# GNN stack on one core: scattering parked edge sums tile by tile with two under way, instead of four at a time

## What is computed

```python
# L0: relational layer, L1: attention, L2: two SAGE layers, L3: GCN
def sage_mean(x, src, dst, W_self, W_neigh, bias, n):
    s = segment_sum(x[src], dst, n)
    cnt = segment_sum(ones, dst, n)
    return x @ W_self.T + (s / maximum(cnt, 1)[:, None]) @ W_neigh.T + bias
# L3
msgs = (x @ W)[src] * (dis[src] * dis[dst])[:, None]
out = segment_sum(msgs, dst, n)
```

## Time and profile before

| | |
|---|---|
| median of 3 runs | 4481.74 us (4466.53 to 4487.24) |
| profiled execution, its own time | 4498.36 us |
| its span | 4496.7 us |
| busy share of the span | PE 65%, PEld 57%, DVE 56%, ACT 43%, POOL 55% |
| three stretches in which scatters and node part run together | 2413 to 2806 us, 3219 to 3692 us, 4084 to 4482 us |

### The profile page before, as it was taken

How to read it: one execution, slowest core, us unless ns; L and a number is a source line. 1 busy time by engine, 2 the same in 40 slices (tenths; PEclk the granted TensorE clock), 3 DMA queues, 4 the chain that set the end, 5 groups by cost and what they waited for, 6 DMA issues and landing times.

```text
span 4496.7 us, 81538 instructions
## 1 busy us (share of the span) xinstructions
PE 2929.0 (65%) x19724; PEld 2566.6 (57%) x19724; DVE 2499.0 (56%) x11513; ACT 1955.0 (43%) x5394; POOL 2473.3 (55%) x2379
## 2 busy tenths in 40 slices
PE   6888887774656563004767777566777665777666
PEld 5887886663555553003655555466666554666666
DVE  5666667885555453883324555323466563445666
ACT  2222325664544442113546555223444444556555
POOL 5565553666788886445554555545444435554444
PEclk9999998998877776556888676778888887889989
DMA  4444436875333333992113767211277771114767
GB/s 160 157 166 156 163 127 192 239 239 157 41 41 41 41 41 75 313 310 77 38 36 112 229 218 220 71 31 34 86 245 239 230 241 49 37 38 137 221 216 220
DMA packets 328251, 638.77 MB, mean 142 GB/s; under 512 B 61072, under 2 KB 89776, under 8 KB 321992
## 3 DMA queue, kind: packets, MB, share of 16 engines
q1 hardware_dynamic: 233406, 501.99, 34.5%
q0 software_dynamic: 90944, 133.85, 13.2%
q10 hardware_dynamic: 3786, 1.65, 0.1%
HBM read 371.35 MB, written 277.50 MB: 144 GB/s over the span
## 4 chain that ended last, share of the span: by engine, by line
PE 16%; DMA 13%; issue 11%; POOL 10%; another core or an unknown queue 4%; DVE 4%; ACT 3%; SPq 0%; POOLq 0%; DVEq 0%; ACTq 0%
DMA sums<-parked,last_i 12%; POOL sums L774 9%; PE bank L1201 6%; PE bank L1197 3%; PE bank L1185 3%; PE bank L1167 2%; DVE out_stats L1665 1%; PE bank L1137 1%; ACT e_h L911 1%; DVE out_mv L1672 1%; ACT out_sd L1072 1%; ACT psum_out L948 1%; DVE n_t L1765 0%; POOL got L739 0%
## 5 line engine op out<-in xcount | busy, mean ns | idle before, releaser
L774 POOL DMA_INDIRECT sums<-parked,last_i x588 | 603.5, 1026 | 702.6 <-DMA sums<-parked,last_i 506.4
L739 POOL DMA_INDIRECT got<-rows,gidx x588 | 602.7, 1025 | 404.8 <-ACT e_h L911 188.4
L948 ACT ACTIVATE psum_out<-bank 128x132 f32<-128x132 f32 x784 | 219.7, 280 | 939.3 <-remote 455.0
L1201 PE MATMUL bank<-psum_out,eq 128*128 128x132 f32 x1568 | 387.2, 332 | 246.0 <-ACT psum_out L948 154.6
L1033 ACT ACTIVATE n_h<-ring 128x128 f32<-128x128 f32 x1176 | 482.9, 482 | 143.7 <-DMA ring<-rows 71.2
L1302 PE MATMUL bank<-ring,ident 128*128 128x128 f32 x2352 | 507.6, 302 | 0.0
L1201 PEld LDWEIGHTS bank<-psum_out,eq 128*128 128x128 f32 x1568 | 271.2, 216 | 306.4 <-ACT psum_out L948 181.9
L1299 PE MATMUL bank<-w_t,n_ht 128*128 128x128 f32 x1568 | 355.7, 353 | 136.1 <-DMA ring<-sums 135.3
L1277 PE MATMUL bank<-ident,n_h 128*128 128x128 f32 x1176 | 226.9, 324 | 330.9 <-ACT n_h L1033 248.2
L1182 PE MATMUL bank<-parked 128*128 128x128 f32 x3136 | 409.7, 283 | 32.7 <-issue 26.1
L1182 PEld LDWEIGHTS bank<-parked 128*128 128x128 f32 x3136 | 386.9, 199 | 41.4 <-issue 40.6
(11 more groups left out here) (182 smaller groups left out, 7292.4 us busy)
## 6 DMA issues: line engine op xcount, KB each, us to landing
ring<-sums SPq DMA_DIRECT2D x392, 264.0 KB
ring<-rows SPq DMA_DIRECT2D x392, 264.0 KB
rows<-ring SPq DMA_DIRECT2D x294, 264.0 KB
ring<-attsums SPq DMA_DIRECT2D x98, 264.0 KB
rowsg<-ring SPq DMA_DIRECT2D x98, 264.0 KB
ring<-rowsg SPq DMA_DIRECT2D x98, 264.0 KB
sums<-parked SPq DMA_DIRECT2D x16, 1584.0 KB
attsums<-parked SPq DMA_DIRECT2D x16, 1584.0 KB
```

Source lines behind the costliest of these rows:

```text
L739: pool.indirect_dma_start(out=got[:, b, j, 0:width], out_offset=None, in_=table[:, :], in_offset=bass.IndirectOffsetOnAxis(ap=gidx[:, b, j ...
L774: pool.indirect_dma_start(out=sums[:, :], out_offset=bass.IndirectOffsetOnAxis(ap=last_i[:, t:t + 1], axis=0), in_=parked[:, t, :], in_off ...
L948: nc.scalar.activation(psum_out[:, b, j, :], bank[4 + j % 2][:, 0:W], ACT.Copy)\
L1201: nc.tensor.matmul(o, lhsT=eq[:, b, j, 1, :], rhs=carried, start=False, stop=True)\
```

## The change

The three parked phases scatter by the tile. Scatter t is issued when the scatter two tiles back, t - 2, has landed. Two semaphores, `tile_scattered0` and `tile_scattered1`, take the tiles in turn and replace `scattered0` and `scattered1` in these phases. After the landing of the fourth tile of a round `rounds_landed` is raised, as before. At the end of a phase both of the last tiles are waited for. The edge part, the node part, the due times and the REL and ATT phases are the same.

```diff
--- before.py
+++ after.py
@@ -356,6 +356,7 @@
         seg_out = Signal(sem("seg_out"), TPR, 2 * TPR)
         counts_taken = Signal(sem("counts_taken"), 1, 2)
         rounds_landed = Signal(sem("rounds_landed"), 1, 1)
+        tile_scattered = [Signal(sem(f"tile_scattered{q}"), 16) for q in range(2)]
         parked_ready = Signal(sem("parked_ready"), 1)
         scattered = [Signal(sem(f"scattered{b}"), 16 * TPR) for b in range(2)]
 
@@ -761,20 +762,19 @@
                             in_=psum_out[:, b, j, :], in_offset=None,
                             bounds_check=bound, oob_is_err=False).then_inc(scattered[b].sem, 16)
 
-                def round_landed(r):
-                    b = r % 2
-                    pool.wait_ge(scattered[b].sem, (parity_first(seg_index(phase), b) + r // 2 + 1) * 16 * TPR)
-                    pool.sem_inc(rounds_landed.sem, 1)
-
-                def scatter_parked(r):
-                    pool.wait_ge(parked_ready.sem, parked_before(phase) + r + 1)
-                    gate(pool)
-                    for j in range(TPR):
-                        t = r * TPR + j
-                        pool.indirect_dma_start(
-                            out=sums[:, :], out_offset=bass.IndirectOffsetOnAxis(ap=last_i[:, t:t + 1], axis=0),
-                            in_=parked[:, t, :], in_offset=None,
-                            bounds_check=bound, oob_is_err=False).then_inc(scattered[r % 2].sem, 16)
+                def tile_landed(t):
+                    pool.wait_ge(tile_scattered[t % 2].sem, 16 * (CHASED.index(phase) * TILES // 2 + t // 2 + 1))
+                    if t % TPR == TPR - 1:
+                        pool.sem_inc(rounds_landed.sem, 1)
+
+                def scatter_tile(t):
+                    if t % TPR == 0:
+                        pool.wait_ge(parked_ready.sem, parked_before(phase) + t // TPR + 1)
+                        gate(pool)
+                    pool.indirect_dma_start(
+                        out=sums[:, :], out_offset=bass.IndirectOffsetOnAxis(ap=last_i[:, t:t + 1], axis=0),
+                        in_=parked[:, t, :], in_offset=None,
+                        bounds_check=bound, oob_is_err=False).then_inc(tile_scattered[t % 2].sem, 16)
 
                 def add_pair(r, q):
                     b = r.mod(DEEP)
@@ -811,9 +811,12 @@
                     else:
                         pool.wait_ge(h_ready.sem, h_ready.credit + normalised_before(phase) + ROUNDS)
                     gate(pool)
-                    for r in range(ROUNDS):
-                        scatter_parked(r)
-                        round_landed(r)
+                    for t in range(TILES):
+                        if t >= 2:
+                            tile_landed(t - 2)
+                        scatter_tile(t)
+                    tile_landed(TILES - 2)
+                    tile_landed(TILES - 1)
 
                 def fetch_dst(r):
```

## The result

| | before | changed |
|---|---|---|
| median of 7 runs | 4482.81 us (4466.53 to 4488.63) | 4516.77 us (4501.63 to 4540.38) |
| ratio | 1 | 1.0079 (95%: 1.0050 to 1.0108) |
| profiled execution, its own time | 4498.36 us | 4502.22 us |

The change made the kernel slower by 0.8%, 34 us between the medians. On a second chip the changed kernel took 4039.93 us (6 executions) against 4015.79 (11): ratio 1.0068 (1.0053 to 1.0084). So the sign and the size hold. The two profiled executions are only 4 us apart. The profiled execution of before is a long one, above all seven of the table, and the one of after a short one: from the last scatter of SAGE0 to the first of SAGE1, outside the changed part, it took 401.6 us where the profile of before has 414.3.

What follows compares the result with a forecast made beforehand. Bound by the loop landing, loads, scatters, landing, not bandwidth or an engine. Two turns a round gave +22, +9 and +22 us in the chases, about +52 on the 4481.74 us median: 4534 us, range 4455 to 4630.

Steps and rivals of the forecast that it cites:

- Turns in series: Chased scatters: two chains of two turns a round replace three 1.28 us spacings and one turn; pays under about 3.8 us.
- The first turn, 4.75 us in SAGE0: Start to next start of a chain's turn under load: 4.75, 4.96 and 4.58 us in SAGE0, SAGE1 and GCN.
- Which tiles meet the loads: Price under load was read from a round's first tile: 3.49, 3.70 and 3.32 us in the chases, 1.93 alone.
- The restart of 0.91 us for every turn: POOL's next scatter starts 0.91 us after a landing: two small increments and 0.77 us of getting going, kept for every turn.
- The second turn, three quarters of the way: A chain's later turn, between lone 3.16 us and the fourth tile's turn, three quarters towards the latter: 3.78, 4.90, 4.00 us.
- The sum: Rounds of 8.53, 9.86 and 8.58 us against 8.09, 9.67 and 8.14; over 49 rounds about +52 us together.
- What stands behind the waits: After the chases everything moves by as much as they lengthen; the later `rounds_landed` taken as nothing, 1 us of 8 at most.
- The signs named: Profile signs: L774 idle spread over nearly all scatters, some 1.1 us each; round lengths; DMA share above 75% or under 62% otherwise.
- A: Rival, two full turns: no second turn in the chases escapes the loads; +130 to +180 us, 4612 to 4662; chance 0.2.
- C: Rival, no difference: turns equal the old rounds, or faster restarts eat half the sum; 4460 to 4504 us; chance 0.21.
- B: Rival, landings shorten: scatters queue behind their own kind, two under way land near lone time; 4322 to 4430 us; chance 0.17.
- the row: Profile rows the forecast followed against the skill's rule: a scatter takes 3.49 us under load, 1.93 alone.

Runs made afterwards that it cites:

- direct_wait: Kernel before, four at a time, with the landing wait directly ahead of the next round's first scatter and the `rounds_landed` increment behind it: 4436.04 us, ratio 0.9824.
- gate_each: Changed kernel with the bare `gate` increment ahead of every scatter instead of every fourth: 4591.39 us, ratio 1.0152 over the kernel before.

## Why the prediction was right

**Turns in series.** Right. The timeline shows two chains with two turns each, one long and one short, and one, three and four under way order themselves as the number of turns in a round does. Without the loads the same change gains 185 us, so its loss hangs on what a turn costs under load.

**The first turn, 4.75 us in SAGE0.** Its landing was 4.10 us where I had 3.84, its restart 0.27 to 0.9 where I had 0.91 throughout: 4.37 us. The mean start-to-start of this turn (second to fourth tile) is 4.40 us in SAGE0, 4.34 in SAGE1 and 4.31 in GCN of the changed kernel.

**Which tiles meet the loads.** Wrong, and without effect on the sum. The price was read from the first tile of a round, which met the loads before. Now the first tile starts before the landing that releases them. Its turn is 3.51, 4.55 and 3.79 us, and the long one of its chain is the second, third tile to next first: 4.64, 5.12 and 4.48 us. The packets in the trace say the same. In SAGE0 the last of a scatter's 32 packets ends, on the mean, 3.52 us after the start of a first tile before and 2.34 us now; for the second and third tile it is now 3.58 and 3.31 us. Each chain still has one turn in the loads and one beside them, so the sum holds for both.

**The restart of 0.91 us for every turn.** This step was wrong. It holds only where increments stand between the wait and the scatter. I had seen the 0.77 us always behind an increment and took it as the engine's own start. The turns without loads and direct_wait show otherwise. In the sum it is up to 0.6 us too much in one of each chain's two turns, 29 us a chase at most; since gate_each gave only some 35 us over three chases, part of it may be hidden by what the tile would meet anyway.

**The second turn, three quarters of the way.** 3.78, 4.90 and 4.00 us; the measured means, from a fourth tile's start to that of the next round's second, are 3.76, 5.34 and 3.97. The chosen weight fitted in SAGE0 and GCN, which is partly luck. No row gave the three quarters. And one of the two ends was read short: I took 1.03 us, the mean of all scatters, for the issue of the fourth tile, whose own mean before is 1.25 in SAGE0. Start to start its turn before was 4.19, 5.41 and 4.25 us, not 3.98, 5.48 and 4.28; with these the same weight gives 3.93, 4.85 and 3.98. In SAGE1, with its longer loads, the second turn is a full one, and the shorter first turn makes up for it: together 9.7 us, not 9.86.

**The sum.** +22, +9 and +22 us forecast for the three chases; the profiles have +5, 0 and +13, and the timed runs +34 in all (+24 on the second chip). The forecast of 4534 us was 17 us too high. The first turns came out 0.35, 0.62 and 0.27 us short of the forecast, although the landing seen above was longer than forecast (4.10 for 3.84 us); so what made them short was the restart. The second turns were right but for SAGE1's, 0.44 us longer, which took most of that back there. And the last round of a chase, some 2 us longer by the tile, wasn't in the sum: an error the other way, of 6 to 7 us in all.

**What stands behind the waits.** Right. On the second chip every stretch outside the chases is within 2 us in the two profiles, and the chases are +3, 0 and +19 us there. On the first chip only the stretch from SAGE0 to SAGE1 differs, by 13 us, in favour of the changed kernel. The second chip doesn't show it, so I take it for the spread of single executions. `rounds_landed`, which is raised a scatter later, was rightly put at nothing: direct_wait delays it as well and is faster all the same.

**The signs named.** They held in part. The mean round was to be 8.3 to 8.8 us in SAGE0 and GCN; it was 8.16 and 8.27 in the changed kernel's profile, and 8.17 and 8.37 on the mean of three, so only GCN's mean lies within: the size per round was put too high. SAGE1's 9.67 lies within 9.6 to 10.2. The idle time ahead of L774 is spread over more scatters, 275 waits for a landing of 1.9 us each in place of 143 of 3.5, and not over nearly all. The DMA share moved to neither rival's side.

**The rivals.** A holds in SAGE1 alone, and there a full second turn was too little to make the round longer; in SAGE0 and GCN the second turn gets out of the loads. C, no difference, is only just out: its limit was 22 us, and the intervals of the two ratios start at 22 us on the first chip and 21 on the second. B's cause is refuted: with one under way a turn in the loads is still 4.5 us, and the first tile's packets end 3.38 us after its start on the mean in SAGE0, against 3.52 with four by the round. The surprise lies on the other side. With four sliding, the packets of a scatter in the software queue end 3.4 to 4.4 us after its start (means of tiles in the three chases), some 0.4 us later than before, and it costs nothing, since no scatter starts right behind it in series. On the rule of the Trainium skill, "DMA: Bandwidth & Descriptors", section "Queues, rings and completion order", that an engine goes round-robin between its queues by the packet, the runs agree with the row and not with the near-lone landing that I drew from the rule: under loads a lone scatter's turn is 4.47 us, and without loads, with two under way, 2.55.

## What to carry to other kernels

When a sequence of transfers waits for its own landings, count the turns in series for a fixed piece of work, and price a turn as issue, landing and restart under the load that it will meet. Under load a sliding window helped here only when it was deep enough to take the turns off the path: two under way replaced three cheap spacings and one turn by two turns and lost 0.8%, four of the same transfers gained 8.8% and brought the DMA share to 92 to 98%. Put a wait that ends late directly ahead of the instruction that it holds, and increments before the wait or behind the instruction.

## What the runs showed of the hardware

An indirect DMA on POOL starts 0.27 us after the landing that it waits for when the wait is directly ahead of it (changed kernel, 2617.68 us), and 0.77 us after the last increment when one stands between (2619.01 us).

A scatter of 128 rows has its last packet 1.86 us after its start while no loads run (mean of SAGE0 in the two kernels with late due times). Under loads the mean is 3.30, 3.89 and 3.12 us in the three chases of before, and 3.69, 4.28 and 3.51 us with four sliding.

The same program ran in 4008 to 4016 us on two chips and in 4483 and 4521 us on others. The chases have the same rounds there (8.04 and 8.09 us in SAGE0), so the edge parts make the difference: the first scatter of SAGE0 comes 253 us earlier on the second chip, and the stretches between the chases are 133 and 101 us shorter. In the edge part of SAGE0 the granted clock of TensorE is 0.87 on the slower chip and 1.00 on the faster one (1.00 is the higher of its two levels, 0.50 the lower). Stretches of the edge part of SAGE0 in the kernel before, on the first chip and, below it, the second:

```profile
2100.00:2350.00 250.00, 180.53 (x1234) 155.89 (x1235) 77.30 (x238) 127.82 (x343) 133.81 (x135) 0.87 0.16 37
```

```profile
1920.00:2120.00 200.00, 172.59 (x1383) 148.98 (x1383) 94.85 (x269) 143.64 (x385) 153.26 (x154) 1.00 0.23 53
```

There POOL issues 0.77 gathers a us on the faster chip and 0.54 on the slower, 30% fewer where the clock is 13% lower. So the clock alone doesn't make up the difference, and whether it is its cause isn't shown. Why the clock is granted differently wasn't tried.
